# Gate products of a node stage cut into 64x64 quarters, and a message pass in another order

## The reference

```python
def _gru_cell(x, h, wih, whh, bih, bhh):
    gi = x @ wih.T + bih
    gh = h @ whh.T + bhh
    ir, iz, inn = jnp.split(gi, 3, axis=-1)
    hr, hz, hn = jnp.split(gh, 3, axis=-1)
    r = jax.nn.sigmoid(ir + hr)
    z = jax.nn.sigmoid(iz + hz)
    n = jnp.tanh(inn + r * hn)
    return (1.0 - z) * n + z * h
...
for _ in range(STEPS):                                  # 6 steps
    msg = jnp.einsum('ei,eio->eo', out[src], w_e)       # a 32x32 matrix per edge
    agg = jax.ops.segment_sum(msg, dst, num_segments=n_nodes) + conv_bias
    m = jax.nn.relu(agg)
    h = _gru_cell(m, h, gru_wih, gru_whh, gru_bih, gru_bhh)
    out = h
```

## Time and profile before

| | |
|---|---|
| median of 3 runs | 7569.24 us (7554.29 to 7577.0) |
| the profiled execution | 7563.81 us, its span 7561.7 us |
| TensorE busy | 5467.3 us, 72% |
| VectorE busy | 4597.3 us, 61% |
| GpSimd busy | 3548.0 us, 47% |
| ScalarE busy | 2487.6 us, 33% |
| mean granted TensorE clock | 0.836 |
| bytes moved | 1039.67 MB, 137 GB/s |

### The profile page before, as it was taken

How to read it: one execution, slowest core, us unless ns; L and a number is a source line. 1 busy time by engine, 2 the same in 40 slices (tenths; PEclk the granted TensorE clock), 3 DMA queues, 4 the chain that set the end, 5 groups by cost and what they waited for, 6 DMA issues and landing times.

```text
span 7561.7 us, 70665 instructions
## 1 busy us (share of the span) xinstructions
PE 5467.3 (72%) x20759; PEld 2497.0 (33%) x20765; DVE 4597.3 (61%) x6813; ACT 2487.6 (33%) x4074; POOL 3548.0 (47%) x3814
## 2 busy tenths in 40 slices
PE   1896888444568755686767676866675796999998
PEld 1443444223233322222222222223354542434343
DVE  5465333123446577697979797883475644666666
ACT  1564333111223311111111121213321254666665
POOL 3677773667655453453535363636206566600000
PEclk9997888665558777798989898987797898999999
DMA  5001555232457588686868687871101001000000
GB/s 167 12 10 46 199 204 205 74 87 79 117 134 175 143 280 296 216 315 227 317 231 314 223 321 245 300 257 42 42 1 28 18 16 27 27 19 25 20 20 20
DMA packets 572067, 1039.67 MB, mean 137 GB/s; under 512 B 112303, under 2 KB 306500, under 8 KB 570789
## 3 DMA queue, kind: packets, MB, share of 16 engines
q1 hardware_dynamic: 458724, 976.22, 37.6%
q0 software_dynamic: 112960, 58.94, 4.6%
HBM read 828.11 MB, written 222.61 MB: 139 GB/s over the span
## 4 chain that ended last, share of the span: by engine, by line
PE 40%; DVE 19%; issue 15%; POOL 13%; DMA 7%; ACT 5%; SPq 1%; DVEq 0%; POOLq 0%; ACTq 0%
POOL gathered L887 10%; DVE ring L2198 5%; PE ps L1407 5%; PE ps L1039 5%; PE ps L1101 5%; PE ps L1189 3%; PE ps L1190 2%; DMA ring<-net 2%; DVE blocks L2198 2%; PE ps L1194 2%; POOL edge_rows L1021 2%; PE ps L1162 2%; DVE w L2245 1%; DVE ring L2240 1%; PE ps L1530 1%
## 5 line engine op out<-in xcount | busy, mean ns | idle before, releaser
L887 POOL DMA_INDIRECT gathered<-table,idx_slot x2156 | 2099.7, 974 | 1090.5 <-issue 548.7
L2198 DVE TENSOR_TENSOR ring<-ring,ps 128x1024 f32<-128x1024 f32 (+2 forms) x1008 | 1058.3, 1081 | 245.1 <-DMA ring<-net 198.2
L1101 PE MATMUL ps<-ring,mats 128*32 128x512 f32 (+2 forms) x4032 | 677.2, 630 | 409.7 <-DVE ring L2198 327.1
L1039 PE MATMUL ps<-mats,gathered 128*128 128x128 f32 x1029 | 204.6, 338 | 594.5 <-DMA gathered<-table,idx_slot 551.3
L879 POOL COPY idx_slot<-idx_row 128x16 int32<-128x16 int32 (+2 forms) x154 | 32.1, 209 | 1118.9 <-SPq L592 1080.8
L1101 PEld LDWEIGHTS ps<-ring,mats 128*32 128x32 f32 x4032 | 155.4, 122 | 896.2 <-issue 565.9
L2265 DVE SCALAR_TENSOR_TENSOR x_block<-ps,bias,blocks 128x512 f32<-128x512 f32 x300 | 224.6, 749 | 366.0 <-PE ps L1194 365.7
L1194 PE MATMUL ps<-ring,wts 128*128 128x512 f32 x600 | 344.4, 657 | 124.8 <-ACT blocks L1771 124.6
L1407 PE MATMUL ps<-w,en 128*128 128x512 f32 (+2 forms) x896 | 381.0, 585 | 0.0
L1039 PEld LDWEIGHTS ps<-mats,gathered 128*128 128x128 f32 x1029 | 136.1, 168 | 741.2 <-DMA gathered<-table,idx_slot 588.9
L1189 PE MATMUL ps<-ring,wts 128*128 128x512 f32 x600 | 334.9, 641 | 40.1 <-ACT ring L1785 31.4
(11 more groups left out here) (310 smaller groups left out, 11886.9 us busy)
## 6 DMA issues: line engine op xcount, KB each, us to landing
ring<-net SPq DMA_DIRECT2D x792, 512.0 KB, 3.9
blocks<-net SPq DMA_DIRECT2D x264, 512.0 KB
net<-ring SPq DMA_DIRECT2D x176, 512.0 KB, 2.9
gathered<-table,idx_slot POOLq DMA_INDIRECT x2352, 3.5
ring<-net SPq DMA_DIRECT2D x144, 256.0 KB, 2.9
table<-w SPq DMA_DIRECT2D x143, 256.0 KB, 2.7
ring<-d_sp SPq DMA_DIRECT2D x100, 256.0 KB, 4.3
x_sp<-x_block SPq DMA_DIRECT2D x79, 256.0 KB
```

Of the source, the lines that this page charges most:

```text
L887: pool.indirect_dma_start(dests(k), None, rows, bass.IndirectOffsetOnAxis(ap=dst[:, k:k + 1], axis=0)).then_inc(done, 16)
L1039: last = nc.tensor.transpose(dst[:, k * P:k * P + P], src[:, k * P:k * P + P], mat["ident"])
L1101: last = mm(message[t * D:t * D + D, 0:wd(i)], adders[2 * m + c], ring[slot][:, c * wd(i):(c + 1) * wd(i)], start=(m == 0 and c == 0), sto ...
L2198: v.tensor_tensor(pair, pair, state, ALU.mult).then_inc(sig["pr"][S_], 1)
```

## The change

The two gate products of the node stage become four: the reset gate's lower and upper diagonal quarter (64 rows by 64 columns of the array), and the update gate's two quarters, written to the other half of `gate_b`'s partitions. The update gate's sigmoid becomes two activations that put the halves back. In P5 TensorE's `variances` move ahead of the second edge sums and `scales` ahead of the third, and VectorE's steps stand behind other multiplies.

```diff
 def gates(n, k, c):
     ready(pe, "hn", c, q.n("hn", c, n, k))
-    mm(gate_a[c], wt["hr"], n_state[c], start=True, stop=True).then_inc(sig["gr"][c], 1)
-    mm(gate_b[c], wt["hz"], n_state[c], start=True, stop=True).then_inc(sig["gz"][c], 1)
+    mm(gate_a[c][lower, :], wt["hr"][lower, lower], n_state[c][lower, :], start=True, stop=True)
+    mm(gate_a[c][upper, :], wt["hr"][upper, upper], n_state[c][upper, :], start=True, stop=True).then_inc(sig["gr"][c], 1)
+    mm(gate_b[c][upper, :], wt["hz"][lower, lower], n_state[c][lower, :], start=True, stop=True)
+    mm(gate_b[c][lower, :], wt["hz"][upper, upper], n_state[c][upper, :], start=True, stop=True).then_inc(sig["gz"][c], 1)
...
     edge_sums4(q, i, 0)
     if more:
         conv_norm(q, i + 1, centre)
+        conv_norm(q, i + 1, variances)
     edge_sums4(q, i, 1)
     if more:
-        conv_norm(q, i + 1, variances)
+        conv_norm(q, i + 1, scales)
     edge_sums4(q, i, 2)
     if more:
-        conv_norm(q, i + 1, scales)
         conv_lin(q, i + 1)
         copies4(q, i + 1)
     edge_sums4(q, i, 3)
...
     ready(act, "gz", c, q.n("gz", c, n, k))
-    f(n_update[c], gate_b[c], ACT.Sigmoid, bias=one_col("nz")).then_inc(sig["z"][c], 1)
+    f(n_update[c][lower, :], gate_b[c][upper, :], ACT.Sigmoid, bias=one_col("nz")[upper, :])
+    f(n_update[c][upper, :], gate_b[c][lower, :], ACT.Sigmoid, bias=one_col("nz")[lower, :]).then_inc(sig["z"][c], 1)
...
 def conv_step(q, i):
-    return {0: lambda: conv_sum(q, i), 1: lambda: conv_scale(q, i), 2: lambda: conv_add(q, i),
-            8: lambda: norm_variance(q, conv_space, i), 9: lambda: norm_root(q, conv_space, i),
-            10: lambda: norm_refine(q, conv_space, i), 13: lambda: norm_apply(q, conv_space, i, [fit(x, i) for x in conv_out])}
+    return {3: lambda: (conv_sum(q, i), conv_scale(q, i)), 4: lambda: conv_add(q, i),
+            7: lambda: norm_variance(q, conv_space, i), 8: lambda: norm_root(q, conv_space, i),
+            9: lambda: norm_refine(q, conv_space, i), 11: lambda: norm_apply(q, conv_space, i, [fit(x, i) for x in conv_out])}
```

## The result

The changed kernel takes 7658.1 us (median, 7647.0 to 7665.8) where the kernel before, run beside it, takes 7561.8: a ratio of 1.0126, 95% interval 1.0109 to 1.0142. The forecast was 7518, with 7465 to 7585 as its range: the change was to gain 0.6% and loses 1.3%. The profiled execution has a span of 7651.7 us against 7561.7.

A forecast was written before the change was run, and what follows sets the result against it. Node stages counted as covered until 6293.86 us, then TensorE-bound; P5 bound otherwise, VectorE busy 26.1 of 34.7 us. 7563.8 - 5 (late node stage) - 45 (P5) = 7513.8, on the median's footing 7519; forecast 7518, range 7465 to 7585.

The forecast's parts named there:

- Part 1a: Node stage's gate products on TensorE as quarters: a call costs 1.2 us instead of 1.72, saving 6.6 us per period.
- turns on a bank: Rival: quarters writing one PSUM bank take turns, 2.9 us a gates call, total 7690 us; chance 0.10.
- two rounds: Rival: the quarter products run in two rounds, 2.07 us a gates call, total 7575 us; chance 0.08.
- the period walked through: Late node stage, followed segment by segment between gates calls: sum -0.2 us a period, taken as -5 us in total.
- Part 1b: Update gate on ScalarE as two 64-partition activations of 0.57 us each: adds 6.8 us of ScalarE per period.
- if the two don't overlap: Upper bound for one half activation of the update gate on ScalarE: 0.69 us; 0.57 was taken.
- one segment: Late node period from step 0 of chain 1 to step 1 of chain 2, where ScalarE leads: net +1.6 us.
- longer slow clock: Rival: TensorE's slow clock after a node-stage stall may last twice as long, +1.4 us a period, 7542; chance 0.12.
- its cover: Early node stage: the next stage doesn't wait for it, since ScalarE stands idle 16.31 us until GpSimd has written `src_ends`.
- Part 2: P5 reordering on TensorE and VectorE: a block takes 30.6 us instead of 34.7, over 11 long blocks -45 us.
- The wait at the block's start: VectorE's load wait opening each P5 block: 1.7 us was to stay, as copies4 waits for the last multiply.
- what was to be seen: Signs: eight records per gates call, activations 0.57 apart, period 74.5 to 75.2 us, P5 blocks 30 to 31 us.

The follow-up runs named there:

- e4: Kernel before with the node stage's four quarter products alone, one full update-gate activation, its halves left swapped: 7537.4 us, ratio 0.9967.
- e3: Kernel before with only the update gate's activation cut into two of 64 partitions, full products, not swapped: 7660.6 us, ratio 1.0124.
- e2: Kernel before with the node stage's quarter products and half activations, message pass as before: 7684.0 us, ratio 1.0163.
- e1: Kernel before with the reordered message pass (P5) alone, node stage as before: 7531.7 us, ratio 0.9961.
- e7: Kernel before with TensorE's new order in P5 alone, VectorE's steps and node stage as before: 7564.6 us, ratio 1.0005.
- e10: Kernel before with quarter products, the update gate's two issued twice, one full activation, halves left swapped: 7593.9 us, ratio 1.0048.
- e5: Kernel before with quarter products and half activations, the update gate's two quarter products issued twice: 7646.4 us, ratio 1.0109.

## Why the prediction was wrong

**Part 1a held.** All four quarters run together; a call takes 1.02 us before an untiled product, forecast 1.2. The rivals with turns on a bank and with two rounds are out. If I price e4's 13 us more of slow clock (16 less 3) at 0.35 to 0.49, they took 4.7 to 6.5 us of its period, and with the 0.8 it gained the quarters are worth 5.5 to 7.3: the forecast 6.6 is in there. That last step is an estimate, as no run had the quarters at the full clock.

**The step that failed is the period walked through**, at +8.5 measured against -0.2. Two things in it were wrong.

- *Part 1b, the half activation at 0.57 us.* It is 0.68 to 0.70, the bound that I had written down as "if the two don't overlap" and not taken. The overlap that makes two full ones 1.25 us long doesn't happen between the two halves (0.68 to 0.70), nor between the second and what follows it (0.71), nor between the reset and the first, swapped one (0.71); the lower half that isn't swapped does overlap with the reset (0.57 in e3). In each of the pairs without the overlap the two activations start at different partitions, on the side they read or the side they write. No run tells whether that is the reason. Where all of it follows directly, a gates call adds 0.98 us to the queue, not 0.57. I had reasoned from TensorE's rows of 64 to ScalarE instead of asking what an activation's time is made of. The Trainium skill (ScalarE: Activation LUTs, What ACT_TABLE_LOAD costs) gives, for tiles of 128 partitions, about 280 ns and 0.833 ns per column, with no term for partitions, and an overlap of about 93 ns back to back. By that an activation of 512 columns is estimated at 0.71 us, which agrees with the record of 0.69 and with the half's 0.68; between full ones the overlap here is 0.12 us (0.69 less 0.57), and in the pairs named it was missing. Direct cost by e3 at equal clock: 3.2 us a period. My walk with 0.57 had shown +1.6 in one segment and gains elsewhere.
- *The granted clock.* The walk priced every product at the full clock, and the rival "longer slow clock" was kept for one stall, at 1.4 us a period. In fact the clock stands at the lower level for up to 25 us a period instead of 3. At 0.35 to 0.49 us each, the 22 us more are 7.7 to 10.8 us. With the halves' 3.2, and less the 5.5 to 7.3 that the quarters would save, that makes 5.4 to 6.8 of the 8.5 (both priced at the same rate). The rest, 1.7 to 3.1 us, is not assigned: swapped halves hold the queue 0.16 us a call longer than e3's, and behind the longer queue TensorE may keep less of what the quarters save; no run separates the two. Each part alone brings the clock down, the quarters (e4: 0.89 to 0.92) and the halves (e3: 0.91 to 0.94 in all periods but one); with both it is 0.85 to 0.90. By what each does it, fewer busy microseconds or more waits, is argued and not shown. The mechanism was on my list, its size was off by a factor of six or so.

**The early node stage was costed at nothing** and its cover named, 16.31 us. The periods there grew as well (two in the middle take 83.5 and 83.9 us instead of 77.4 and 75.8), so that the last square root activation starts 25.2 us later (633.5 against 608.3), and used the cover up: the activation behind `src_ends` starts at 696.4 us, and at 690.9 in e2, where e1, e7 and e10 have it at 679.2, 683.0 and 684.1 and the kernel before at 684.7; that the changed kernel and e2, alike up to there, differ by 5.5 us shows how far to trust this. Of the 10.9 us at P5's start not all need be from this, since that start varies by some us between kernels that are alike up to there (2602.8 in e1, 2612.4 in e7). It fell for the same reason as the late stage: with a period of -0.2 no cover was needed.

**Part 2 was right in mechanism; its size is 31 us where 45 were forecast (e1), of which the traces place 23 to 28 in P5.** The waits before multiply 8 and L2117 are gone, the DMA share is 0.88, and the block in the changed kernel is 31.4 us (below), where 30.6 was forecast:

```profile
2776.20 1.22 DVE L2201 TENSOR_TENSOR ring<-ring,ps 128x1024 f32<-128x1024 f32 x1 [2.99 <-DMA ring<-net]
...
2802.30 2.38 DVE L2201 TENSOR_TENSOR blocks<-blocks,ps 128x1024 f32<-128x1024 f32 x2 [1.30 <-DMA blocks<-net]
...
2807.57 1.22 DVE L2201 TENSOR_TENSOR ring<-ring,ps 128x1024 f32<-128x1024 f32 x1 [2.89 <-DMA ring<-net]
```

The wait at the block's start is 2.9 us, not the 1.7 I had left there, and a new one of 1.3 to 2.0 us for the loads stands before multiply 14. The forecast took the share 0.88 to be worth 32.3 us a block and then chose 30.6, against its own row.

**Of what was to be seen** the eight records, the missing wait before multiply 8 and conv_out waiting over 1 us (1.77) came; the half activations 0.57 apart, the period of 75 and TensorE busy 62 did not, and P5's block stayed just outside what was named (31.4 us at a share of 0.88).

## What to carry to other kernels

Products made cheaper on TensorE can lower its clock: here the quarters alone brought it from 0.98 to about 0.90, and in one kernel the same period took 78.3 us at full clock and 82.6 at 0.94. So price a saving once at each level, and look for what will newly make TensorE wait. Cutting an activation by partitions cost a full one and its overlap (0.82 to 0.98 us a call), by columns 0.27; cut by columns if it must be cut, and undo a swap on the engine that has room on the path. When two engines hand a chain back and forth, move both orders or neither: here each alone gave 0 and +38 us, both -31.

## What the runs showed of the hardware that was not expected

- Four 64x64 products, two from the lower and two from the upper rows, with one of each writing the same PSUM bank, start within 0.02 us and run together.
- An activation of 64 partitions and 512 columns lasts as long as one of 128 (0.68 and 0.69 us). Where it starts to read or to write at another partition than its neighbour, the two don't overlap: pitch 0.68 to 0.71, where full ones, and a full one with an unswapped lower half behind it, have 0.57.
- Redundant products made a kernel faster: e5 has 10 us of products more per period than e2 and is 38 us shorter, its clock 0.94 to 1.00 instead of 0.85 to 0.90.
- A period could settle in a cycle: e5 repeats 78.3, 81.5 and 82.6 us, with the clock at 1.00, 0.96 and 0.94. The unchanged node stage has it too: in e7 its period ranges from 74.8 us at 0.98 to 79.2 at 0.91, with the same instructions.
